# First moments of the last two rows of x taken by ScalarE instead of VectorE, in a one-core attention and expert-lookup kernel

## The reference, cut to what matters

```python
def _layernorm(x, axis=-1, eps=1e-05):
    m = jnp.mean(x, axis=axis, keepdims=True)
    v = jnp.var(x, axis=axis, keepdims=True)
    return (x - m) / jnp.sqrt(v + eps)

xn = _layernorm(x, axis=-1)
s = _L0_attn_ref(xn, ...)          # compressed, selected (top 64 of 512 by score) and window attention, gated, normed
g = _silu(_L0_ffn_ref(xn, ...))    # product-key lookup: top 16 of 32 keys twice, top 16 of the 256 pairs, gelu, softmax
x = x + s * g
```

## Time and profile before

| | |
|---|---|
| median of 3 runs | 301.37 us (300.31 to 302.27) |
| the profiled execution, its own time | 301.44 us |
| its span in the profile | 299.7 us |
| mean granted TensorE clock | 0.957 of full |
| busy: PE, VectorE (DVE), ScalarE (ACT), POOL | 244.5, 271.6, 241.2, 228.9 us |
| chain that ended last, by engine | DVE 64%, PE 15%, POOL 9%, ACT 3%, issue 8% |

### The profile page before, as it was taken

One profiled execution on the slowest core, in us unless ns is written; L12 is line 12 of the kernel. 1 busy time (PEld: TensorE's weight loads), 2 busy tenths in 40 slices (PEclk: granted clock), 3 DMA queues, 4 the chain that ended last, 5 costly groups with the idle time before them and its releaser, 6 DMA issues.

```text
span 299.7 us, 7849 instructions
## 1 busy us (share of the span) xinstructions
PE 244.5 (82%) x1512; PEld 175.9 (59%) x1512; DVE 271.6 (91%) x2581; ACT 241.2 (80%) x1031; POOL 228.9 (76%) x354
## 2 busy tenths in 40 slices
PE   0699796969788898899888988898899888977591
PEld 0635242757567575767565756575767565756481
DVE  5679999986999999999999999999999999995464
ACT  3235568437999899899998999899899989998913
POOL 8886411425886988998899889978997899788871
PEclk9999999958999999799999999999799999999958
DMA  8920000000000000000010001000100010001011
GB/s 172 258 63 1 1 3 0 0 3 0 1 1 3 1 1 3 19 20 3 1 37 2 3 0 37 2 2 1 39 0 3 2 36 2 3 1 37 0 35 35
DMA packets 11111, 6.26 MB, mean 21 GB/s; under 512 B 1332, under 2 KB 10552, under 8 KB 11064
## 3 DMA queue, kind: packets, MB, share of 16 engines
q1 hardware_dynamic: 9736, 5.12, 6.5%
q10 hardware_dynamic: 1328, 0.66, 1.1%
HBM read 3.68 MB, written 2.10 MB: 19 GB/s over the span
## 4 chain that ended last, share of the span: by engine, by line
DVE 64%; PE 15%; POOL 9%; issue 8%; ACT 3%; POOLq 0%; DVEq 0%
DVE rest L1086 23%; DVE top L1095 14%; DVE top L1075 13%; DVE last L1119 6%; POOL squareT L466 2%; DVE slot_gap L1104 1%; PE sim L1417 1%; PE f_bank L1410 1%; PE c_bank L1410 1%; PE sim L1380 1%; DVE st L1010 1%; DVE den L1061 1%; PE s_bank L1403 1%; POOL rstd L431 1%; POOL wgt L479 1%
## 5 line engine op out<-in xcount | busy, mean ns | idle before, releaser
L1086 DVE MATCH_REPLACE8 rest<-top,sim 128x32 f32<-128x32 f32 x512 | 85.6, 179 | 0.2 <-issue 0.2
L1095 DVE MAX8 top<-rest 128x8 f32<-128x32 f32 x512 | 53.7, 176 | 0.7
L1075 DVE MAX8 top<-sim 128x8 f32<-128x32 f32 x496 | 50.9, 177 | 2.2 <-PE sim L1417 2.2
L767 ACT ACTIVATE prob<-drop 128x50 f32<-128x50 f32 x184 | 42.2, 250 | 0.0
L466 POOL TENSOR_TENSOR squareT<-sideT 100x512 bf16<-100x512 bf16 x31 | 32.8, 1057 | 11.9 <-ACT sideT L702 11.9
L451 POOL TENSOR_TENSOR past<-gap,last 128x400 f32<-128x400 f32 x31 | 26.8, 863 | 18.4 <-DVE last L1119 18.4
L1086 DVE MATCH_VALUE_LOAD rest<-top,sim 128x8 f32 x512 | 40.5, 79 | 0.3
L767 ACT ACTIVATION_READ_ACCUMULATOR prob<-drop 128x1 f32 x184 | 38.1, 207 | 0.0
L473 POOL TENSOR_TENSOR drop<-gap,out_by 128x400 f32<-128x400 f32 x31 | 32.0, 1032 | 3.9 <-ACT out_by L693 3.9
L1417 PE MATMUL sim<-sim_w,xT_all 128*128 128x512 f32 x64 | 33.9, 612 | 0.8 <-issue 0.8
L479 POOL TENSOR_TENSOR wgt<-prob,rden 128x400 f32<-128x400 f32 x30 | 25.6, 855 | 8.9 <-DVE rden L1065 8.9
(11 more groups left out here) (263 smaller groups left out, 752.8 us busy)
## 6 DMA issues: line engine op xcount, KB each, us to landing
out<-y_sb SPq DMA_DIRECT2D x7, 256.0 KB, 2.2
x_sb<-in_L_attn_hidden_states SPq DMA_DIRECT2D x2, 256.0 KB, 4.2
fwq_sb<-in_L_ffn_Wq ACTq DMA_DIRECT2D x2, 256.0 KB, 6.0
x_sb<-in_L_attn_hidden_states SPq DMA_DIRECT2D x1, 512.0 KB, 6.0
wc_sb<-in_L_attn_Wc SPq DMA_DIRECT2D x1, 256.0 KB
out<-last_y SPq DMA_DIRECT2D x2, 128.0 KB, 1.8
wo_sb<-in_L_attn_Wo SPq DMA_DIRECT2D x1, 192.0 KB
keys_sb<-in_L_ffn_keys ACTq DMA_DIRECT2D x1, 128.0 KB, 3.7
```

The costliest lines, as they stand in the source:

```text
L767: last = nc.scalar.activation(prob[d][:, h, :], drop[:, h, :], ACT.Exp, scale=-1.0, accum_out=den[d][:, h:h + 1])
L1075: last = nc.vector.max(top[d][:, v, 0:8], sim_bank[d][:, bass.ts(v, KEYS)])
L1086: last = nc.vector.match_replace(out=rest[:, v, :], in_to_replace=top[d][:, v, 0:8], in_values=sim_bank[d][:, bass.ts(v, KEYS)], imm_value ...
L1095: last = nc.vector.max(top[n % 2][:, v, 8:16], rest[:, v, :])
```

## The change

ScalarE gets a function `row_moments(b)` for rows 6 and 7 and runs it for row 6 in its front loop behind the copy of row 2, for row 7 behind the copy of row 3 and ahead of `norm_rows(5)`. For each row it makes four Identity passes that sum each tile over its features, one small pass that turns the four sums into negative means, and four Square passes with that as the bias, whose sums are the squared deviations. `row_stats(6)` and `row_stats(7)` leave VectorE. POOL waits for the squares instead of for VectorE's moments in the last group, takes variance + eps from the sum of squares, and multiplies by the negative mean, so that its negation step is not needed there.

```diff
--- before.py
+++ after.py
@@ -165,6 +165,7 @@
         xT_all = sb("xT_all", [P, TILES * P])
         st1 = sb("st1", [P, TILES, 6])
         mv1 = sb("mv1", [P, TILES, 2])
+        sum1, nmean1, sq1 = (sb(n, [P, TILES]) for n in ("sum1", "nmean1", "sq1"))
         var1, rstd1, prod1, nmr1 = (sb(n, [P, TILES]) for n in ("var1", "rstd1", "prod1", "nmr1"))
         geluT = sb("geluT", [TWO, TILES * P])
         z_sb = sb("z_sb", [4 * B, L])
@@ -253,6 +254,7 @@
         stats1, mean1, norm1_ready, xn_done = (
             sem("stats1"), sem("mean1"), sem("norm1_ready"), [sem("xn_done_even"), sem("xn_done_odd")])
         pool_step = sem("pool_step")
+        late_sums, late_means, late_squares = (sem(n) for n in ("late_sums", "late_means", "late_squares"))
         xt_full, xt_out, side_full, side_out = (sem(n) for n in ("xt_full", "xt_out", "side_full", "side_out"))
         zw_done, z_ready, z_done, gate_ready = (sem(n) for n in ("zw_done", "z_ready", "z_done", "gate_ready"))
         unit_full, unit_out = sem("unit_full"), sem("unit_out")
@@ -290,6 +292,8 @@
 
         POOL_NORMS = [1, 2, 4, 6]
         ACT_NORMS = [3, 5, 7]
+
+        ACT_MOMENTS = [6, 7]
         assert sorted([0] + POOL_NORMS + ACT_NORMS) == list(range(B))
 
 
@@ -424,15 +428,22 @@
 
             for g, (b0, b1) in enumerate(NORM_GROUPS):
 
-                pool.wait_ge(mean1, b1)
                 t = slice(TB * b0, TB * b1)
-                nc.gpsimd.tensor_scalar(var1[:, t], mv1[:, t, 1], 1e-5, None, ALU.add).then_inc(pool_step, 1)
+                if b0 < ACT_MOMENTS[0]:
+                    pool.wait_ge(mean1, b1)
+                    nc.gpsimd.tensor_scalar(var1[:, t], mv1[:, t, 1], 1e-5, None, ALU.add).then_inc(pool_step, 1)
+                else:
+                    pool.wait_ge(late_squares, len(ACT_MOMENTS))
+                    nc.gpsimd.tensor_scalar(var1[:, t], sq1[:, t], 1.0 / D, 1e-5, ALU.mult, ALU.add).then_inc(pool_step, 1)
                 pool.wait_ge(pool_step, 3 * g + 1)
                 nc.gpsimd.tensor_tensor(rstd1[:, t], var1[:, t], neg_half[:, t], ALU.pow).then_inc(pool_step, 1)
                 pool.wait_ge(pool_step, 3 * g + 2)
-                nc.gpsimd.tensor_tensor(prod1[:, t], mv1[:, t, 0], rstd1[:, t], ALU.mult).then_inc(pool_step, 1)
-                pool.wait_ge(pool_step, 3 * g + 3)
-                nc.gpsimd.tensor_scalar(nmr1[:, t], prod1[:, t], -1.0, None, ALU.mult).then_inc(norm1_ready, 1)
+                if b0 < ACT_MOMENTS[0]:
+                    nc.gpsimd.tensor_tensor(prod1[:, t], mv1[:, t, 0], rstd1[:, t], ALU.mult).then_inc(pool_step, 1)
+                    pool.wait_ge(pool_step, 3 * g + 3)
+                    nc.gpsimd.tensor_scalar(nmr1[:, t], prod1[:, t], -1.0, None, ALU.mult).then_inc(norm1_ready, 1)
+                else:
+                    nc.gpsimd.tensor_tensor(nmr1[:, t], nmean1[:, t], rstd1[:, t], ALU.mult).then_inc(norm1_ready, 1)
                 pool.wait_ge(norm1_ready, g + 1)
                 for b in range(b0, b1):
                     if b in POOL_NORMS:
@@ -659,6 +670,24 @@
                               ffn_wq[bass.ts(half, HEADS * DKEY), :].rearrange("(h c) d -> c h d", h=HEADS)
                               ).then_inc(fwq_in, 16)
 
+            def row_moments(b):
+
+                k = ACT_MOMENTS.index(b)
+                act.wait_ge(x_in[3], 16)
+                tiles = range(TB * b, TB * b + TB)
+                for t in tiles:
+                    last = nc.scalar.activation(spare[:, 0, t % TB, :], x_sb[:, t, :], ACT.Identity,
+                                                accum_out=sum1[:, t:t + 1])
+                last.then_inc(late_sums, 1)
+                act.wait_ge(late_sums, k + 1)
+                nc.scalar.activation(nmean1[:, TB * b:TB * b + TB], sum1[:, TB * b:TB * b + TB], ACT.Copy,
+                                     scale=-1.0 / D).then_inc(late_means, 1)
+                act.wait_ge(late_means, k + 1)
+                for t in tiles:
+                    last = nc.scalar.activation(spare[:, 1, t % TB, :], x_sb[:, t, :], ACT.Square,
+                                                bias=nmean1[:, t:t + 1], accum_out=sq1[:, t:t + 1])
+                last.then_inc(late_squares, 1)
+
             def norm_rows(b):
 
                 act.wait_ge(norm1_ready, 1 + [b0 <= b < b1 for b0, b1 in NORM_GROUPS].index(True))
@@ -730,6 +759,8 @@
                     nc.scalar.activation(ahead[0:TWO, :], c_bank[0:TWO, P:P + TWO], ACT.Sign,
                                          bias=half_col[0:TWO, 0:1]).then_inc(ahead_done, 1)
                     take_topT(0)
+                if b + 4 in ACT_MOMENTS:
+                    row_moments(b + 4)
                 if b + 2 in ACT_NORMS:
                     norm_rows(b + 2)
                 if b == 5:
@@ -1196,9 +1227,6 @@
                 if n >= 1:
                     gaps_of_thirds(n - 1)
                     last_gaps(n - 1)
-                if n == 0:
-                    row_stats(6)
-                    row_stats(7)
                 if n == 2:
                     select_tokens(3)
                     invert_gates()
```

## The result

The changed kernel took 303.98 us (median of 13 runs, 301.13 to 307.25), the one before 301.25 (13 runs, 299.28 to 305.36). The ratio is 1.0093, 95% interval 1.0052 to 1.0135. A second set of twelve runs gave 303.58 against 301.51, ratio 1.0061 (1.0027 to 1.0095). Ratios and means in this text take in the runs that lie within 1.5% of the fastest of their kernel, medians take in all, also four executions of 332 to 1195 us (one of them of the kernel before). So the changed kernel is 0.6 to 0.9% slower. The forecast was 302.2 with a range of 300.7 to 303.8, and the median of the first set lies just above it, that of the second just inside.

The account below looks back on a forecast made before the run. The prediction took the chain through POOL's norm and TensorE's transposes of row 6 to the attention scores, not VectorE, as the bound: 301.44 us + 0.75 from ScalarE's queue = 302.2 us, range 300.7 to 303.8.

Parts of the forecast that it names:

- What bounds the front: Up to about 70 us the chain to row 0's attention scores binds, not VectorE; its 2.27 us saved becomes idle time.
- A row of moments, 2.93 us: On ScalarE, sums, negative means and squares of one row: 1.20 + 0.02 + 0.27 + 1.44 = 2.93 us.
- the order part: ScalarE's queue delays row 5's norm and copies, so TensorE's transposes of row 6 start at 32.88 instead of 32.13: +0.75 us.
- The second rival: Moments cost only 2.4 us a row and ScalarE does not bind; transposes of row 6 at 31.8, 301.1 us; chance 0.12.
- The wait of 2.2 us on TensorE: Before the transposes of row 5, TensorE idles from 27.44 to 29.68, 2.24 us, for ScalarE's norm.
- POOL doesn't decide: POOL's norm of row 6 is done by about 32.3, before TensorE starts the transposes of row 6 at 32.88.
- the granted clock stays at 1.00 in the gap: TensorE's clock keeps its higher level in the new wait before row 5's transposes, so the forecast adds nothing for it.
- the first rival: TensorE's clock falls to 0.50 in the new gap, costing 3.4 to 5.0 us: 305.6 to 307.2 us; chance 0.11.
- the fall at 59 us: In the kernel before, TensorE's granted clock fell to 0.50 at 59.0 us and stayed down 10.1 us.
- The stretch behind 57 us only shifts as a whole: What stands ahead of 59 us shifts by 0.75 us; VectorE's wait for the first scores stays about 3.4 us.

Follow-up runs that it names:

- the filled version: Changed kernel plus two extra 512-column matmuls, results unused, in TensorE's gap before the transposes of row 5: 302.46 us against 301.51 before, ratio 1.0039.
- The version with one extra matmul: Changed kernel plus one extra 512-column matmul, result unused, in TensorE's gap before the transposes of row 5: 303.46 us against 301.49 before, ratio 1.0047.
- the made gap: Kernel before, with only TensorE made to wait ahead of the transposes of row 5 until POOL's last group is ready: 306.02 us against 302.36, ratio 1.0113.
- moments_early: Kernel before, with the moments of rows 6 and 7 still on VectorE but right behind those of rows 4 and 5: 301.7 us against 301.49, ratio 1.0006.
- the filled gap: Kernel before, TensorE made to wait ahead of the transposes of row 5, with two extra matmuls in that wait; second set 301.91 us against 302.19, ratio 0.9993.

## Why the prediction was wrong

- *What bounds the front* held. VectorE's saving was idle time at L1135 and L1203; in the three traces of the changed kernel, one of them with its gap filled, the end came 3.9, 2.1 and 1.1 us later, the transposes of row 6 3.92, 2.81 and 1.10.
- *A row of moments, 2.93 us*: measured 3.09. From SBUF a sum took 0.29 from start to start and a square 0.385, where the rows of PSUM plus 16 ns gave 0.27 and 0.36. Twice 0.16 is the 0.3 us by which row 5 was late (29.96 against 29.68), and the order part became 1.10 us instead of 0.75 (33.23 in the filled version against 32.88). The second rival, moments of 2.4 us, fell. From the figures of the Trainium skill ("ScalarE: Activation LUTs", What ACT_TABLE_LOAD costs) the passes by themselves are estimated at 293 and 386 ns; the trace has 296 and 386 in the median, so it agrees. The trace has in addition an accumulator read of 0.19 us behind each pass. The 2.4 us that the prediction gives for a row by these figures is itself high: 4 x 0.20 + 4 x 0.29 and 0.29 for the means make an estimate of 2.25.
- *The wait of 2.2 us on TensorE*: 2.52, for the instruction named. *POOL doesn't decide*: its norm of row 6 ended at 30.79 + 1.74 = 32.53, before TensorE was free even in the filled version.
- **The step that failed**, besides the moments that were 0.16 us a row too cheap, is the choice that the granted clock stays at 1.00 in the gap, with 0.11 for the first rival. I leaned on a stretch of the kernel before with 1.84 us of TensorE work in 3.4, at 1.00. The new stretch has half that:

```profile
26.80:30.20 3.40, 0.88 (x4) 0.44 (x4) 3.32 (x38) 3.40 (x13) 1.66 (x2) 0.86 0.01 2
```

The clock fell at 29.3 us, near the end of this stretch. In the second trace the same stretch had 0.72 us of TensorE work and kept 1.00, and the fall came at 30.3. The argument set the new gap beside a stretch with twice the work, and gave little weight to the fall at 59 us, which it names and which had come with 2.69 us of work in 3.4. The rival's mechanism was right and its price too high for the median: it took the 10.1 us of the fall at 59 as its length, and the falls in the front measured 6.7 and, in the second trace (0.86 over the same 12 us), 3.4 us.

What the clock took can be said in two ways. In the traces the transposes of row 6 were 1.7 and 2.8 us late by it, beside 1.10 by order. Over the second set of runs the half clock was 28.2 - 24.6 = 3.6 us more, by the line of 0.25 worth 0.9 us; with 1.10 of order that makes 2.0 us, where the means differ by 303.37 - 301.50 = 1.9. (Half of 3.6 instead would make 2.9, too much.) For the filled version the order alone, 1.10, stands against 1.1. Runs with equal half clock give some 0.9 us for the order: at 25.8 us ten runs of before took 301.22 to 301.53, and two of the changed kernel beside them, at 25.8 and 25.9, took 302.26 and 302.34. So of the 1.9 us, by estimate, about 1.0 is order, of which 0.75 was forecast, and about 0.9 is the clock, which the forecast put at nothing. The first set is 2.8 us slower in its means; the clock of its runs of before is not on record.

- *The stretch behind 57 us only shifts as a whole*: not in every run. In the first trace its fall lasted 13.9 us (0.67 over 21 us) against 10.1, in the second 10.1. VectorE's wait at L1203 came to 5.3 and 4.8 us instead of 3.4.

## What to carry to other kernels

Before work goes to an engine that looks idle, look at what its idle scraps stand ahead of. Here they fed TensorE, and the room was one row of moments, not two. A new wait on TensorE must be priced twice, for the delay and for the clock that it may take from everything behind it; here each came to about 1 us over the runs, and in the two traces the second was the larger. And with a clock that differs from run to run, a trace is one draw: read the order of events from it, and the price from many runs.

## What was not expected

- Extra matmuls with no use made a kernel faster: by over 1% in the one with the made gap, and by 1.1 us in the medians of the changed one, which is not clear of noise.
- The version with one extra matmul had a trace of 299.5 us of span and a median of 303.46 us. The span of before was 299.7 us: a verdict from the trace would have had the wrong sign.
- Kernels with the transposes of row 6 1.1 us earlier (moments_early) or 1.36 later (the filled gap) both came out at the time of before. At this size the time at half clock, 21 to 32 us in the means, moves the result as much as the order does.
